# Block sums spread over two tiles, 71 routed tiles for 72, and a reordered last stage in a one-core attention and expert kernel

## The reference, cut to what matters

```python
x = L0_attn_x                                   # (2, 2048, 512), f32
xn = _layernorm(x, axis=-1)
x = x + _L0_attn_ref(xn, ...) + _L0_ffn_ref(xn, ...)

def _L0_attn_ref(...):                          # 16 heads of 32 columns, latent width 128
    c = layernorm over the latent of einsum('bhsd,hld->bhsl', xh, Wdkv), times ln_g, plus ln_b
    q_lat = einsum('bhsd,hdl->bhsl', xh, absorbed);  scores = q_lat . c / sqrt(L), causal, softmax
    oh = einsum('bhst,bhtd->bhsd', w, v);  out = (oh by Wo_h) @ Wo.T + bo

def _L0_ffn_ref(x, gate_w, gate_b, expert_w, expert_b):
    gate_logits = jnp.einsum('nsd,de->nse', x, gate_w) + gate_b
    _, top_idx = jax.lax.top_k(gate_logits, K)                 # K = 2 of 8 experts
    all_out = jax.nn.relu(jnp.einsum('nsd,edo->nseo', x, expert_w) + expert_b)
    return jnp.take_along_axis(all_out, top_idx[..., None], axis=2).mean(axis=2)
```

## Time and profile before

| what | value |
|---|---|
| time, median of 3 runs | 1564.26 us (1561.05 to 1564.79) |
| the profiled execution's own time | 1571.43 us |
| its span in the trace | 1569.7 us |
| PE busy, share of the span | 1500.6 us, 96% |
| DVE busy | 1138.1 us, 73% |
| ACT busy | 900.6 us, 57% |
| POOL busy | 581.1 us, 37% |
| bytes moved by DMA | 198.06 MB, mean 126 GB/s |

### The profile page before, as it was taken

One profiled execution on the slowest core, in us unless ns is written; L12 is line 12 of the kernel. 1 busy time (PEld: TensorE's weight loads), 2 busy tenths in 40 slices (PEclk: granted clock), 3 DMA queues, 4 the chain that ended last, 5 costly groups with the idle time before them and its releaser, 6 DMA issues.

```text
span 1569.7 us, 42867 instructions
## 1 busy us (share of the span) xinstructions
PE 1500.6 (96%) x12544; PEld 807.4 (51%) x12545; DVE 1138.1 (73%) x2385; ACT 900.6 (57%) x1629; POOL 581.1 (37%) x725
## 2 busy tenths in 40 slices
PE   5899989999999999999999999999999999999998
PEld 3888845444444444444444444444444455554443
DVE  6888788887777777777777777777777344444477
ACT  2677756666666666666666666666666633333200
POOL 3444411323454454533223222322223366666400
PEclk9999989999999999999999999999999999999999
DMA  7688932232222322223222232223222256654499
GB/s 192 196 265 269 264 102 60 64 92 80 68 70 67 87 78 72 65 69 93 74 70 65 75 93 69 72 62 89 82 72 65 73 174 219 196 165 162 157 406 354
DMA packets 156337, 198.06 MB, mean 126 GB/s; under 512 B 45280, under 2 KB 94560, under 8 KB 155904
## 3 DMA queue, kind: packets, MB, share of 16 engines
q1 hardware_dynamic: 114720, 98.23, 21.8%
q10 hardware_dynamic: 27936, 61.38, 12.4%
q0 software_dynamic: 13632, 37.87, 7.4%
HBM read 109.13 MB, written 63.12 MB: 110 GB/s over the span
## 4 chain that ended last, share of the span: by engine, by line
PE 73%; DVE 11%; DMA 6%; issue 4%; SPq 2%; POOL 1%; ACT 1%; another core or an unknown queue 1%; DVEq 0%; ACTq 0%; POOLq 0%
PE PS L1321 29%; PE PS L1449 29%; PE PS L1498 11%; DVE pm L1026 5%; DMA arena<-in_x 4%; PE PS L1480 2%; DVE mx L1031 1%; POOL arena L628 1%; POOL arena L634 1%; DVE w_lo L1263 1%; DVE w_lo L1261 1%; SPq L439 1%; DVE stats L935 1%; DVE mx L1030 1%
## 5 line engine op out<-in xcount | busy, mean ns | idle before, releaser
L1026 DVE TENSOR_REDUCE pm<-PS 128x1 f32<-128x512 f32 (+3 forms) x1280 | 717.0, 602 | 193.7 <-PE PS L1321 179.3
L883 ACT ACTIVATE arena<-PS 128x512 f32<-128x512 f32 (+1 forms) x1152 | 613.4, 574 | 294.0 <-PE PS L1321 273.2
L1321 PE MATMUL PS<-arena 97*64 97x512 f16 (+7 forms) x5120 | 693.2, 352 | 24.4 <-DVE pm L1026 22.4
L1449 PE MATMUL PS<-arena 128*33 128x512 f32 (+3 forms) x2560 | 634.1, 530 | 1.0 <-POOL arena L656 1.0
L1321 PEld LDWEIGHTS PS<-arena 96*64 96x64 f16 (+1 forms) x5120 | 329.1, 110 | 413.2 <-DVE pm L1026 136.7
L656 POOL TENSOR_SCALAR_AFFINE_SELECT arena<-arena 128x256 f32<-128x256 f32 (+1 forms) x256 | 111.5, 436 | 539.4 <-ACT arena L883 538.3
L1449 PEld LDWEIGHTS PS<-arena 128*33 128x33 f32 x2560 | 159.0, 111 | 80.7 <-POOL arena L656 1.7
L1498 PE MATMUL PS<-w_hi,arena 128*128 x576 | 172.7, 382 | 5.4 <-ACT arena L902 4.3
L902 ACT ACTIVATE arena<-PS 128x1024 f16<-128x1024 f32 x72 | 73.3, 1024 | 153.0 <-remote 118.0
L1321 PE MATMUL PS<-later,deny 128*64 128x128 f16 x1024 | 144.6, 221 | 0.0
L1239 DVE SCALAR_TENSOR_TENSOR arena<-PS,eb_bc 128x512 f32<-128x512 f32 x72 | 49.8, 692 | 122.8 <-remote 56.3
(11 more groups left out here) (174 smaller groups left out, 1278.9 us busy)
## 6 DMA issues: line engine op xcount, KB each, us to landing
comb_hl<-arena SPq DMA_DIRECT2D x256, 64.0 KB
w_hi<-expert_rows ACTq DMA_DIRECT2D x32, 512.0 KB, 7.4
arena<-q_pieces ACTq DMA_DIRECT2D x90, 128.0 KB
arena<-k_pieces ACTq DMA_DIRECT2D x90, 128.0 KB
v_rows<-w_lo SPq DMA_DIRECT2D x8, 1056.0 KB, 7.4
arena<-in_x SPq DMA_DIRECT2D x16, 512.0 KB, 5.8
xn_rows<-arena SPq DMA_DIRECT2D x16, 512.0 KB, 6.2
q_pieces<-w_hi SPq DMA_DIRECT2D x32, 256.0 KB, 5.4
```

Of the source, the lines that this page charges most:

```text
L883: a.activation(probs[kk % 4][:, a_ * CH:a_ * CH + w], PS[:, s2_bank(k, x), 0:w], ACT.Exp, scale=SCALE).then_inc(s["exp_done"], 1)
L1026: v.reduce_max(pm[:, c, r, p:p + 1], PS[:, S1_BANK[n], 0:w], AX).then_inc(s["s1_done"], 1)
L1321: last = t.matmul(PS[h:h + P // 2, bank, cols], lhsT[:, h:h + P // 2], rhs, start=start, stop=stop)
L1449: last = t.matmul(PS[rows_, 6 + c % 2, CH - wds[a]:CH], v_sb[pu % 2][:, j + a, :], probs[pk % 4][:, a * off:a * off + wds[a]], start=p_ in ...
```

## The change

It has three parts. (1) In the first stage the statistics of tile 3 and the aggregation move from the step of tile 2 to the step of tile 3. (2) `PT` is 71, not 72: one expert tile less; the leftovers of the loops (one tile on ACT, three on DVE and on PE) are written out. (3) In the fourth stage the projections go to banks (q + 2) mod 8, so that the first six do not wait for the last expert tile's DVE operation (`half_done`) and the seventh and eighth do; DVE adds x and the two expert rows of tile n + 1 before it adds the projection of tile n; and PE may overwrite a bank when that last addition is done (`acc_done`).

```diff
--- before.py
+++ after.py
@@ -39,7 +39,7 @@
     NT = B * ST
     HPB = P // HD
 
-    PT = -(-(NT * TOP + NE - 1) // 2) * 2
+    PT = NT * TOP + NE - 1
     MS = 64.0
     AHEAD_G = 4
     LOWEST = -3.0e38
@@ -908,9 +908,11 @@
             with act.Fori(BESIDE + 1, PT // 2) as i:
                 for u in range(2):
                     turned(i * 2 + u, u)
+            for n in range(PT // 2 * 2, PT):
+                turned(n, n % 2)
 
             for q in range(Y_RING):
-                act.wait_ge(s[f"y_st{q}"], 16 * PT // Y_RING)
+                act.wait_ge(s[f"y_st{q}"], 16 * len(range(q, PT, Y_RING)))
             act.wait_ge(s["z_ps"], count(PT))
             for n in range(NT):
                 q, at = n % OUT_RING, (n // B + n % B * ST) * P * TOP
@@ -1061,8 +1063,8 @@
                                            scalar=1.0 / WS, in1=q_hi[:, :, tl * P:(tl + 1) * P],
                                            op0=ALU.mult, op1=ALU.subtract).then_inc(s["ql_done"], 1)
                 at = ahead_tile(i, p, ROWS_AHEAD + 4, more)
-                if at and at[2] < CT - 1:
-                    means(at[1], at[3], (at[2],) if at[2] < CT - 2 else (CT - 2, CT - 1))
+                if at:
+                    means(at[1], at[3], (at[2],))
                 at = ahead_tile(i, p, QUERIES_AHEAD, more)
                 if at:
                     n, u, tl, ii = at
@@ -1251,20 +1253,30 @@
             with dve.Fori(2, PT // Y_RING) as i:
                 for q in range(Y_RING):
                     rows(i, q)
-
-            def sums(n):
+            for q in range(PT % Y_RING):
+                rows(PT // Y_RING, q)
+
+            def rows_sum(n):
                 m, q = divmod(n, OUT_RING)
                 lnk, cnt = linker(dve, s["dveE"], n * 2)
                 dve.wait_ge(s[f"out_done{q}"], count(m * 16))
                 dve.wait_ge(s[f"xc_in{q}"], count((m + 1) * 16))
+                dve.wait_ge(s[f"yg_in{q}"], count((m + 1) * 16))
+                lnk(v.tensor_tensor(acc[q], xc[q], y_g[q][:, 0:E], ALU.add))
+                v.tensor_tensor(acc[q], acc[q], y_g[q][:, E:2 * E], ALU.add).then_inc(s["dveE"], 1)
+
+            def add_projected(n):
+                q = n % OUT_RING
+                dve.wait_ge(s["dveE"], count(n * 2 + 2))
                 dve.wait_ge(s["proj_ps"], count(n + 1))
-                lnk(v.scalar_tensor_tensor(out=acc[q], in0=PS[:, q, :], scalar=1.0 / WS, in1=xc[q], op0=ALU.mult, op1=ALU.add))
-                dve.wait_ge(s[f"yg_in{q}"], count((m + 1) * 16))
-                lnk(v.tensor_tensor(acc[q], acc[q], y_g[q][:, 0:E], ALU.add))
-                v.tensor_tensor(acc[q], acc[q], y_g[q][:, E:2 * E], ALU.add).then_inc(s["acc_done"], 1)
-
+                v.scalar_tensor_tensor(out=acc[q], in0=PS[:, (q + 2) % OUT_RING, :], scalar=1.0 / WS, in1=acc[q],
+                                       op0=ALU.mult, op1=ALU.add).then_inc(s["acc_done"], 1)
+
+            rows_sum(0)
             for n in range(NT):
-                sums(n)
+                if n + 1 < NT:
+                    rows_sum(n + 1)
+                add_projected(n)
 
 
         @block.tensor
@@ -1484,10 +1496,10 @@
             pairs = ((0, 0), (1, 0), (0, 1))
             pe.wait_ge(s["stage_free"], count(BH))
 
-            def experts(i, more):
-                for q in range(AHEAD_G):
+            def experts(i, tiles, more):
+                for q in range(tiles):
                     n, u = i * AHEAD_G + q, q % 2
-                    if q < AHEAD_G - 1 or more:
+                    if q < tiles - 1 or more:
                         turn(n + 1, i + (q + 1) // AHEAD_G, (q + 1) % AHEAD_G)
                     e = pe.value_load(expert_of[0:1, ds(n, 1)], min_val=0, max_val=NE - 1)
                     pe.wait_ge(s["gT_done"], count(n + 1))
@@ -1503,23 +1515,25 @@
             pe.wait_ge(s["exp_done"], count(NX * BH))
             turn(0, 0, 0)
             pe.wait_ge(s["ot_done"], count(NC * BH))
-            with pe.Fori(0, PT // AHEAD_G - 1) as i:
-                experts(i, True)
-            experts(PT // AHEAD_G - 1, False)
+            assert PT % AHEAD_G
+            with pe.Fori(0, PT // AHEAD_G) as i:
+                experts(i, AHEAD_G, True)
+            experts(PT // AHEAD_G, PT % AHEAD_G, False)
 
 
             pe.wait_ge(s["gT_done"], count(PT))
-            pe.wait_ge(s["half_done"], count(PT))
-
             pe.wait_ge(s["o_out"], count(16 * BH))
             pe.wait_ge(s["comb_in"], count(16))
             def project(m, q, again):
                 u, at = q % B, q // B * P
+                bank = (q + 2) % OUT_RING
                 if again:
-                    pe.wait_ge(s["dveE"], count((m * OUT_RING + q - OUT_RING) * 2 + 1))
+                    pe.wait_ge(s["acc_done"], count((m - 1) * OUT_RING + q + 1))
+                elif bank < 2:
+                    pe.wait_ge(s["half_done"], count(PT))
                 terms = [(k, z, y) for k in range(KB) for z, y in pairs]
                 for q_, (k, z, y) in enumerate(terms):
-                    last = t.matmul(PS[:, q, :], attnT[:, u * KB + k, ds(m, 1), z, at:at + P].rearrange("p o q -> p (o q)"),
+                    last = t.matmul(PS[:, bank, :], attnT[:, u * KB + k, ds(m, 1), z, at:at + P].rearrange("p o q -> p (o q)"),
                                     comb_hl[:, y, k, :], start=q_ == 0, stop=q_ == len(terms) - 1)
                 last.then_inc(s["proj_ps"], 1)
 
```

## The result

| what | before | after |
|---|---|---|
| time, median of 5 runs each | 1563.08 us (1561.05 to 1564.79) | 1555.18 us (1553.07 to 1556.52) |
| ratio, 95% interval | | 0.9949 (0.9939 to 0.9960) |
| profiled execution's own time | 1571.43 us | 1553.07 us |
| span in the trace | 1569.7 us | 1551.3 us |
| PE busy | 1500.6 us | 1494.5 us |

A forecast was written before the change was run, and what follows sets the result against it. It took a chain through DVE, SP's queue and the load of x to bound the rows, PE the experts, and PE, DMA and DVE nearly level the last stage; 3.04 + 3.0 + 1.0 = 7.0 us gave 1557.3 us, range 1552.5 to 1562.3.

The forecast's parts named there:

- What bounds the rows: Rows: a chain through DVE, SP's queue and the load of x sets a chunk's 19.57 us, not PE.
- One tile less: Experts: one tile's turning and multiplying leave PE's list, 3.04 us shorter, with 3.0 and 3.2 as ends.
- Balanced means: Rows: moved statistics and aggregation fill 0.60 us of DVE waits in each of six chunks; 3.0 us shorter taken.
- the lead-in: Rows, ahead of the loop's six chunk pairs: the moved statistics were to gain about 0.3 us there.
- The bound from above: Rows: most the moved statistics could gain, PE's removable waits plus idle fill on two chunks: 6 us.
- B: Rival: PE sets the last stage's end and the rows gain all they can; 11.4 us shorter, chance 0.11.
- Where the wait for x stays: Rows: DVE's wait for x in tile 2's step stays, since tile 2's own statistics still need it.
- The last stage: Last stage: PE's 0.94 us gap goes, but loads of x hold the end; 1.0 us shorter, ends 2.9 and -0.7.
- C: Rival: only the tile counts, the load of x keeps chunk length, DMA the end; 3.0 to 4.5 us shorter, chance 0.26.
- D: Rival, rows: moved work delays PE and the load of x 1.05 us six times; 5.4 us longer, chance 0.05.
- The sum: Whole kernel: 3.04 + 3.0 + 1.0 = 7.0 us shorter, forecast 1557.3 us.

The follow-up runs named there:

- the half-loaded rows: The changed kernel without the load of each token's second expert row in the last stage (output wrong); ratio 0.9931 to before, 10.8 us shorter.
- the means alone: The kernel before with only tile 3's statistics and the aggregation moved to tile 3's step; ratio 0.9972, 4.4 us shorter.
- the kernel with the means later still: The kernel before with each tile's statistics, and the aggregation after tile 3, put behind the low half of the keys; ratio 1.0024, 3.8 us longer.

## Why the prediction was right or wrong, point by point

- **What bounds the rows** (a chain through DVE, SP's queue and the load of x, not PE): right; POOL's two operations, which the prediction left out of it, are on the chain too, 17.6% from 100 to 125 us. The load issued earlier gained 4.2 us more, and only then PE became the bound (40.00 of 40 us).
- **One tile less**, 3.04 us: right; 3.0 alone, and 3.0 to 3.3 for each of two more. Nothing was lost behind the loops: projections start 0.21 us behind the last expert matmul's start.
- **Balanced means**, 3.0 us: the size was too small; it measured 4.4. The mechanism, DVE's two waits filled, agrees with the timelines, but no run isolates it from PE's wait for the keys. Two steps of the sum failed. I priced DVE's two waits at their printed idle, 0.37 + 0.23 = 0.60 us. Their price is the difference of start to start: queries' low half to reciprocal 1.05 us with the wait (the earlier trace rows has its end, 125.83) against 0.60 without (123.22 to 123.82, the same operation ahead of the statistics in after); reciprocal to the keys' low half 0.49 against 0.14; keys' low half to the next 0.68 against 0.54. That is 0.45 + 0.35 + 0.14 = 0.94 us a chunk: operations that don't wait start before their neighbour ends. Over five chunks the trace has 159.29 - 60.89 = 98.40 us before and 156.92 - 63.03 = 93.89 after, 0.90 each; over all traces the five chunks are 97.4 to 98.6 us with the rows as before and 93.6 to 94.2 with the change, 0.8 each. The sixth step gains as much again behind the last pair, which would make 5 us; in after 1.0 us of it is lost in the lead-in (63.03 - 26.02 = 37.0 us against 60.89 - 24.86 = 36.0). The lead-in is 36.0 to 37.2 us in the traces with the rows as before and 36.1 to 37.0 with the change, so the 0.3 us that I gave it isn't there. Second, I took 0.9 us off for DMA engines that were 0.93 busy. They went on to 0.95 and 0.99. The bound from above was also added up wrongly: PE's waits and two idle fills are 3.8 + 2 x 0.60 = 5.0, not 6 or rival B's 5.5.
- **Where the wait for x stays**: right (2.7 us in four, for 3.5).
- **The last stage**, 1.0 us: about right, 0.8 by time (-0.6 to 2.2) and 1.3 by the traces. PE's gap went; the first `acc_done` comes 3.34 us behind the first expert rows (1472.40 to 1475.06 + 0.68), where it was 1.41 (1489.21 to 1489.93 + 0.69), 1.9 later for the 2.1 forecast; the loads keep the end, 1.74 us behind PE. The x of tile 26 did not land as before: its wait ends 1536.08 - 1468.70 = 67.4 us behind the first load of expert rows, where it was 1554.68 - 1485.61 = 69.1, so 1.7 sooner. That may be the one load less ahead of it, for which I had 1.28; no run shows it by itself. The DMA windows show 413, 411 and 410 GB/s from 1480 to 1540, as the earlier trace rows. The Trainium skill (DMA: Bandwidth & Descriptors, Where 436 GB/s comes from) says that a limit of about 358 GB/s on the memory's side binds such transfers; that is again not borne out in this stage. The packets, which no row of the prediction shows, are in the DMA view of after: 4608 for the 16.78 MB of expert rows and 8064 for the 14.68 MB of x and results, so those of the queue that lands first are twice as large.
- **The rivals.** B (11.4 us: PE sets the end): its last-stage half is refuted by the half-loaded rows, its half on the rows is nearer the truth (4.4, between my 3.0 and its 5.5). C (only the tile) is refuted by the means alone, 4.4 us (3.0 to 6.0). D (slower, by 1.05 us a chunk): refuted by 0.11 us in tile 3's step; yet another place for the same work can lose time, as the kernel with the means later still shows (3.8 us, some 2 of them in the rows).
- **The sum**: 7.0 forecast, 7.9 measured; 3.0 + 4.4 + 0.8 = 8.2 from the parts. Setting the profiled execution 7.2 us above the median aside by subtraction was sound. The likely reason is now visible: the pause, 8.9 us in that trace, and the first expert tile at the lower clock, 1.7 us. I had both in the trace of before and didn't see them, since its PE was 96% busy and nothing in the sum asked for ACT's rows or the clock there. The 0.9 us between 7.0 and 7.9 are less than the interval (1.6 us to either side); the rows, 1.4 too small, are the only term that was clearly off.

## What to carry to other kernels

- A wait that other work can fill is worth the difference of start to start with and without it, not the idle that the profile prints: here 0.94 us for a printed 0.60.
- Work put between two dependent steps of another engine is cover. Look in which steps of a pattern it is missing before looking at who waits longest; moved a few instructions further, the same work gained nothing and lost some (+3.8 against -4.4 us, though 1.7 of the 3.8 is the clock by its trace).
- Before comparing two profiled executions, cut both into stages and compare each with the timed difference. A stage that moved more than its change can explain (13.6 us for one tile) holds other things, here two: 8.9 us of pause and 1.7 us of clock.

Of the versions tried that give the right output for any data, the changed kernel with x issued one step earlier is the fastest: 0.9922 and, with the copies written out too, 0.9908 of before; 69 tiles (0.9907) serve only data that fill no more.

## What the runs showed of the hardware

- On one chip ACT, DVE and POOL stop in the expert stage at releases that the profile can't place: ACT 28 to 31 times for about 3.9 us, once in two tiles, 7 to 9 us of time in all. On another chip the same instructions show none. A turn of ACT's loop isn't the cause.
- A DMA share of 0.93 to 0.95 left room: with loads issued earlier the same stretch moved 301 GB/s at 0.99.
- PE meets the first expert tile after idles of about 1.0 and 0.7 to 0.8 us in every trace; in four of the fourteen its granted clock is then 0.53 to 0.59 over 3.6 us, and that tile takes 1.7 us longer.
